# Second attention of a four-layer recurrent stack: queries projected once, two heads per matmul

## The chip, the cores and the metric

The kernel runs on one core of one Trainium2 chip. The metric is device microseconds of one execution, here the median of three runs. Engines are named as in the profile: PE is TensorE, DVE is VectorE, ACT is ScalarE, POOL is GpSimd, SP is SyncE, which issues the transfers.

## The reference, cut to what matters

The model has four layers. In each, an attention and a feed-forward part read the layer-normalised rows, and the product of the first and the gated second is added to the rows. There are 8192 rows of 128 numbers, worked on in 16 batches of 512. The change touches the attention of the second layer:

```
def _L1_attn_ref(x, Mq, Mk, Mv):
    HEADS = 8
    K_SIZE = 64
    B, C, _ = x.shape
    H, K = (HEADS, K_SIZE)
    V = Mv.shape[1] // H
    q = (x @ Mq).reshape(B, H, C, K)
    k = (x @ Mk).reshape(B, H, C, K)
    v = (x @ Mv).reshape(B, H, C, V)
    scores = jnp.einsum('bhqk,bhck->bhqc', q, k).reshape(B * H, C, C)
    att = jax.nn.softmax(scores / jnp.sqrt(jnp.float32(K)), axis=1)
    att4 = att.reshape(B, C, H, C)
    out = jnp.einsum('bqhc,bhcd->bqhd', att4, v)
    return out.reshape(B, C, H * V)
...
x = x + s * g
xn = _layernorm(x, axis=-1)
s = _L1_attn_ref(xn, L1_attn_Mq, L1_attn_Mk, L1_attn_Mv)
```

Here x is (16, 512, 128). The queries are reshaped without a transpose, so a head of the reference is a group of 64 consecutive rows with all 512 columns, and the softmax runs over the query axis. The kernel counts these groups as g and the eight blocks of 64 columns as s; in this document, as in the few words of the change, "head" means such a block of 64 columns.

## The kernel before, in words

`program` runs the phases of the four layers one after the other. The second attention is `paired_attention_phase`. Its loop goes over n = -1 to 16; the body of n computes the scores of batch n, prepares batch n + 1 and finishes batch n - 1. Each body has STEPS = 16 steps s = 8 rho + g. In a step TensorE issues two score matmuls that share one moment of the array (L582: key rows 0 to 63 on partitions 0 to 63, and 64 to 127 on the other half), each with 512 moving columns of queries, into one of two PSUM tiles of two banks, `scores_ps[s % 2]`. VectorE takes the maximum of both halves (`col_max`, L477), ACT the exponentials with their sums (`exps`, L437), VectorE the reciprocal (`invert`, L483), and GpSimd scales the probabilities in place (`scale_probs`, L404). The scores of step s wait for the exponentials of step s - 2, which free their PSUM tile.

Between the scores TensorE does the work of `misc_use` and `products`, in this order by step. Step 0 turns the normalised rows of the next batch (L111), which ACT copies to `rows.xT` and, twice side by side, to `xT_twice`. `project_k` (L613) makes keys in four parts, at the steps in K_AT; VectorE copies them (L488). `project_q` (L608) makes queries, one head of 64 columns at a time, at the steps in Q_AT; ACT scales and copies them into `q` (L427). The weights `wq` hold every head twice, so one matmul writes the same head into partitions 0 to 63 and 64 to 127, and both score matmuls find it on their half. Steps 9 and 10 turn the output of the batch before (L624), step 15 projects the values (L618). `products` (L601) adds up the weighted values of the first half of the keys in steps 10 to 13 and of the second half in steps 2 to 5 of the next body. All projections and turned outputs share two PSUM banks, `misc[s % 2]`; before a matmul overwrites one, TensorE waits for the copy that read its last content.

VectorE also forms the rows of batch n + 2 in steps 1 to 6: `sum_picks` (L500), `scale_s` (L505), `gate_s` (L509), which waits for a tanh on ACT (L447), `sum_x` (L514), then the moments (L92), and in step 11 `normalise` (L102). These stand in its queue between the maxima. The queue of SP holds, in each body: the four loads of batch n + 3, one weight load for the next phase, the store of the attention output of batch n - 1, a wait until it has landed, and the store of the rows of batch n + 2.

Of the kernel before, what the change touches and what calls it, by code (L numbers as in the profile page):

```python
# [163 lines left out]
def paired_attention_weights(nc, ctx, dram):  # L164
    S, W = 8, 64
    ahead = Ahead(nc, ctx, "a1", {"ident": [P, P], "wq": [D, S, 2, W], "wk": [D, 2, 2, 2, W], "wv": [D, D]})
    ident, wq, wk, wv = ahead.take("ident wq wk wv")
    ahead.loads = [(ident[:], dram["ident"]), (wv[:], dram["L1_Mv"])]
    ahead.loads += [(wq[:, :, twice, :], dram["L1_Mq"].rearrange("d (s w) -> d s w", s=S)) for twice in range(2)]
    k_columns = dram["L1_Mk"].rearrange("d (rho half a w) -> d rho half a w", rho=2, half=2, a=2)  # L170
    ahead.loads += [(wk[:, :, a, half, :], k_columns[:, :, half, a, :]) for a in range(2) for half in range(2)]
    return ahead
# [110 lines left out]
def paired_attention_phase(nc, tag, before_dram, x_dram, s_dram, routes, batches, ahead, following):  # L283
# [14 lines left out]
    Q_AT = {3: 0, 4: 1, 5: 2, 6: 3, 7: 4, 8: 5, 11: 6, 12: 7}  # L298
    K_AT = {1: 0, 2: 1, 13: 2, 14: 3}
    OUT_AT = {9: 0, 10: 1}  # L300

    with nc.cleanup_on_exit(), ExitStack() as ctx:
# [14 lines left out]
        q = sb("q", [P, 2, G, S, W])  # L317
# [14 lines left out]
        q_projected, q_ready = sem("q_projected"), sem("q_ready")  # L332
# [28 lines left out]
        def _(sp):  # L361
# [9 lines left out]

            load_parts(0)
# [3 lines left out]
            def body(j, n):  # L376
                if n <= LAST - 3:
                    load_parts(n + 3)
                following.load(sp, n - 1)
                if n >= 1:  # L380
                    b = j.plus(-1)
                    sp.wait_ge(s_ready, b.of(2, 2))
                    sp.dma_start(s_rows[b.number()], s_out[:]).then_inc(s_stored, 16)
                    sp.wait_ge(s_stored, b.of(16, 16))
                    sp.sem_inc(s_free, 1)
                if n <= LAST - 2:
                    store_x(n + 2)
# [29 lines left out]
        def _(act):  # L417
# [7 lines left out]
            def keep_q(b, buf, s, bank):  # L425
                act.wait_ge(q_projected, b.of(S, s + 1))
                act.activation(q[:, buf, :, s, :], grouped(bank), ACT.Copy,  # L427
                               scale=1.0 / math.sqrt(W)).then_inc(q_ready, 1)
# [22 lines left out]
            def body(j, n):  # L451
                for s in range(STEPS):
# [4 lines left out]
                    if n <= LAST - 1:  # L457
                        if s == 0:
                            keep_twice(j.plus(1))
                        if s in Q_AT:  # L460
                            keep_q(j.plus(1), (n + 1) % 2, Q_AT[s], misc[s % 2])
# [7 lines left out]
        def _(dve):  # L469
# [49 lines left out]
            def body(j, n):  # L519
                if n >= 0:  # L520
                    chain.restart()
                for s in range(STEPS):
# [19 lines left out]
                    if n <= LAST - 1 and s in K_AT:  # L542
                        keep_k(j.plus(1), (n + 1) % 2, K_AT[s], misc[s % 2])
# [3 lines left out]
                    if n >= 1 and s in OUT_AT:  # L547
                        at = OUT_AT[s]
                        dve.wait_ge(out_turned, j.of(2, at - 1))
                        if at == 0:  # L550
                            dve.wait_ge(s_free, j.of(1, 0))
                        dve.tensor_copy(s_out[:, :, at * 64:(at + 1) * 64].rearrange("p c (s d) -> p c s d", s=4),
                                        misc[s % 2][:].rearrange("p (c s d) -> p c s d", c=NC, s=4)[:, :, :, 0:DV]
# [15 lines left out]
        def _(pe):  # L569
            pe.sem_inc(products_done, 2)  # L570

            def scores(j, n, s):
                rho, g = divmod(s, G)
                if s == 0:
                    pe.wait_ge(q_ready, j.of(S, S))
# [51 lines left out]
            def misc_use(j, n, s):  # L627
# [7 lines left out]
                if s == 1 and nxt:  # L635
# [3 lines left out]
                    project_k(b, 0, misc[1])  # L639
                if s == 2 and nxt:  # L640
                    pe.wait_ge(twice_ready, b.of(1, 1))
                    project_k(b, 1, misc[0])
                if s == 3 and nxt:
                    pe.wait_ge(k_ready, b.of(4, 1))
                if s == 4 and nxt:
                    pe.wait_ge(k_ready, b.of(4, 2))
                if s in (5, 6, 7, 8) and nxt:
                    pe.wait_ge(q_ready, b.of(S, Q_AT[s - 2] + 1))
                if s in (11, 12) and nxt:
                    if n >= 1:  # L650
                        pe.wait_ge(s_ready, j.of(2, OUT_AT[s - 2] - 1))
                    else:
                        pe.wait_ge(q_ready, b.of(S, Q_AT[s - 4] + 1))
                if s in Q_AT and nxt:
                    project_q(b, Q_AT[s], misc[s % 2])
                if s in OUT_AT and n >= 1:
                    if nxt:
                        pe.wait_ge(q_ready, b.of(S, Q_AT[s - 2] + 1))
# [5 lines left out]
                    turn_out(n, OUT_AT[s], misc[s % 2])  # L664
                if s in (13, 14) and nxt:
                    pe.wait_ge(q_ready, b.of(S, Q_AT[s - 2] + 1))
                    project_k(b, K_AT[s], misc[s % 2])
                if s == 15 and nxt:
                    pe.wait_ge(k_ready, b.of(4, 4))
# [3418 lines left out]
```

## Time and profile before

| | |
|---|---|
| time, median of 3 runs | 6118.59 us (6117.81 to 6122.44) |
| span of the profiled execution | 6107.7 us |
| second attention, first scores to first scores of the last batch | 1260.03 to 1922.77 us |
| one batch of it | 44.06 us |
| PE busy over the span | 5688.7 us (93%) |
| DVE / ACT / POOL busy | 4318.9 (71%) / 3844.6 (63%) / 2914.7 us (48%) |
| DMA, mean over the span | 36 GB/s |

The page gives one profiled execution; a line such as L608 is a line of the kernel before. The second attention is about an eighth of the span, and its batches repeat, so it is read from one batch in order of time. In the rows below, a matmul in this number format is recorded as two matmuls, and a pair of score matmuls as four.

### The profile page before, as it was taken

What the parts mean: (1) busy time and instruction counts of PE and PEld (TensorE: products, weight loads), DVE (VectorE), ACT (ScalarE), POOL (GpSimd) and SP (SyncE); (2) the same over time, 40 slices, a digit from 0 to 9 for tenths busy, and PEclk for the clock granted to TensorE, in tenths of its full rate; (3) what the DMA queues carried; (4) which work ended last, traced back from release to release, by engine and by line L of the source; (5) the groups of instructions that cost most, each with busy time, mean ns of one, the idle gap of its engine ahead of it and who ended that gap; (6) DMA issues with size and microseconds to landing.
All of it is one profiled execution on the core that took longest, in us unless ns stands there. A gap on an engine that the chain in (4) does not pass through costs nothing. (4 is left out here: it accounts for less than half of the span.)

```text
span 6107.7 us, 102241 instructions
## 1 busy us (share of the span) xinstructions
PE 5688.7 (93%) x33833; PEld 3009.1 (49%) x33833; DVE 4318.9 (71%) x9755; ACT 3844.6 (63%) x8213; POOL 2914.7 (48%) x2774
## 2 busy tenths in 40 slices
PE   8999999779998999999999989999999999987868
PEld 3444444422222566666666634444444444445558
DVE  4555555177886777777788768888888888867655
ACT  2444444256665677777777757777777777756436
POOL 1224325457776766766666533323323323224458
PEclk9999999899999999999999989999999999999989
DMA  2001001211110111111111110000000000013123
GB/s 48 22 22 38 28 15 45 67 57 47 33 36 18 42 33 35 36 33 39 41 43 46 37 26 11 13 20 11 13 17 14 13 14 16 11 40 105 60 96 97
DMA packets 303981, 219.33 MB, mean 36 GB/s; under 512 B 27858, under 2 KB 279636, under 8 KB 302948
## 3 DMA queue, kind: packets, MB, share of 16 engines
q1 hardware_dynamic: 289332, 182.51, 11.2%
q0 software_dynamic: 12544, 29.71, 1.4%
q8 instruction: 275, 4.51, 0.3%
q14 instruction: 246, 2.02, 0.1%
q10 hardware_dynamic: 1584, 0.59, 0.0%
HBM read 97.11 MB, written 73.87 MB: 28 GB/s over the span
## 5 line engine op out<-in xcount | busy, mean ns | idle before, releaser
L3883 PE MATMUL a_scores_ps<-a_kT,a_q_mixed 128*128 128x512 f32 x2048 | 1046.4, 593 | 3.7 <-ACT a_probs L3695 3.1
L3893 PE MATMUL a_acc_ps<-a_probsT,a_v_post 128*128 128x512 f32 x2048 | 1042.8, 592 | 0.4 <-DVE a_probsT L3788 0.4
L3695 ACT ACTIVATE a_probs<-a_scores_ps,a_neg_max 128x512 f32<-128x512 f32 x1024 | 702.3, 686 | 429.5 <-DVE a_neg_max L3778 419.9
L3778 DVE TENSOR_REDUCE a_neg_max<-a_scores_ps 128x1 f32<-128x512 f32 x1024 | 692.9, 677 | 199.9 <-PE a_scores_ps L3883 194.2
L3788 DVE STREAM_TRANSPOSE a_probsT<-a_probs 128x512 f32<-128x512 f32 x1024 | 715.6, 699 | 136.6 <-PE a_acc_ps L3893 112.2
L3700 ACT ACTIVATE a_probs<-a_probs,a_inv_sum 128x512 f32<-128x512 f32 x1024 | 727.7, 711 | 0.8 <-DVE a_inv_sum L3783 0.8
L3096 DVE TENSOR_REDUCE a_neg_max<-a_pair_ps 128x2 f32<-128x1024 f32 (+3 forms) x512 | 417.5, 823 | 354.3 <-PE a_pair_ps L3192 347.8
L2901 ACT ACTIVATE a_probsT<-a_pair_ps 128x1024 f32<-128x1024 f32 (+3 forms) x512 | 359.0, 703 | 485.9 <-PE a_pair_ps L3205 469.0
L3893 PEld LDWEIGHTS a_acc_ps<-a_probsT,a_v_post 128*128 128x128 f32 x2048 | 389.0, 190 | 490.9 <-issue 488.8
L3883 PEld LDWEIGHTS a_scores_ps<-a_kT,a_q_mixed 128*128 128x128 f32 x2048 | 384.4, 190 | 476.6 <-issue 440.6
L3644 POOL TENSOR_TENSOR a_q_mixed<-a_qT,a_pre 128x512 f32<-128x512 f32 x248 | 250.0, 1040 | 759.7 <-PE a_scores_ps L3883 759.7
L404 POOL TENSOR_TENSOR a_probs<-a_probs,a_inv_sum 128x1024 f32<-128x1024 f32 x256 | 488.4, 1918 | 207.1 <-DVE a_inv_sum L483 206.9
L2862 POOL TENSOR_SCALAR_AFFINE_SELECT a_probsT<-a_probsT 128x256 f32<-128x256 f32 x512 | 209.6, 410 | 682.2 <-ACT a_probsT L2901 680.0
L437 ACT ACTIVATE a_probs<-a_scores_ps,a_neg_max 128x512 f32<-128x512 f32 x512 | 347.1, 684 | 241.9 <-DVE a_neg_max L477 240.7
L3652 POOL TENSOR_TENSOR a_v_post<-a_v,a_post 128x2048 f32<-128x2048 f32 x60 | 271.6, 4538 | 456.7 <-PE a_acc_ps L3893 332.6
L3192 PE MATMUL a_pair_ps<-a_k,a_q 32*128 32x512 f32 (+3 forms) x2048 | 436.5, 504 | 0.0
L3205 PE MATMUL a_pair_ps<-a_q_less,a_k 32*128 32x256 f32 (+3 forms) x2048 | 410.3, 487 | 27.9 <-DVE a_neg_max L3096 19.5
L978 ACT ACTIVATE f_probs<-f_s_ps,f_neg_max,f_q_norms 128x128 f32<-128x128 f32 x1024 | 386.2, 469 | 35.6 <-DVE f_neg_max L1126 35.1
L477 DVE TENSOR_REDUCE a_neg_max<-a_scores_ps 128x2 f32<-128x1024 f32 x256 | 312.7, 1222 | 126.0 <-PE a_scores_ps L582 120.9
L912 POOL TENSOR_TENSOR f_cos_part<-f_cos_part,f_sin_part 128x512 f32<-128x512 f32 x128 | 162.3, 1268 | 381.0 <-DVE f_sin_part L1111 381.0
L582 PE MATMUL a_scores_ps<-a_q,a_k 64*128 64x512 f32 x1024 | 293.2, 650 | 17.8 <-ACT a_probs L437 16.3
L1290 PE MATMUL f_k_ps<-f_w_qkv,f_hT 128*128 128x512 f32 x512 | 267.2, 604 | 6.7 <-DVE f_sin_part L1111 3.9
(420 smaller groups left out, 11852.0 us busy)
## 6 DMA issues: line engine op xcount, KB each, us to landing
f_v_even<-f_v_odd SPq DMA_DIRECT2D x224, 130.0 KB, 2.4
a_v<-a_v_rows SPq DMA_DIRECT2D x256, 64.0 KB
f_x_tiles<-routed_x SPq DMA_DIRECT2D x72, 193.0 KB
attention_out<-a_s_out SPq DMA_DIRECT2D x48, 256.0 KB, 2.3
routes_y_rows<-a_zeros SPq DMA_DIRECT2D x32, 256.0 KB
a_parts<-routes_y_rows SPq DMA_DIRECT2D x32, 256.0 KB, 3.5
f_x<-x_after SPq DMA_DIRECT2D x32, 256.0 KB, 2.8
f_gx<-x_after SPq DMA_DIRECT2D x32, 256.0 KB, 3.1
```

Of the source, the lines that this page charges most:

```text
L404: pool.tensor_tensor(units, units, inv_sum[:, s % 2].unsqueeze(2).to_broadcast([P, 2, S * W]), ALU.mult).then_inc(scaled, 1)
L978: last = act.activation(probs[:, hh, hp, :], score_ps[hh][:, hp * P:(hp + 1) * P], ACT.Exp, bias=neg_max[:, hh, hp:hp + 1], scale=q_norms[ ...
L2901: act.activation(probsT[:, g % NPT, 2 * rp:2 * rp + 2, 0:m], slot[:, :, 0:m], ACT.Exp).then_inc(probsT_ready, 1)
L3096: dve.tensor_reduce(neg_max[:, t, c, at:at + 33:32], ring[pair_of(n, 2 * s)][:, :, 0:m], AX.X, ALU.max, negate=True).then_inc(max_ready, 1)
L3192: last = pe.matmul(slot[:, a, 0:(c + 1) * P], q[r:r + 32, t, c * P:(c + 1) * P], k[r:r + 32, buf, t, p, 0:(c + 1) * P], start=False, stop= ...
L3205: last = pe.matmul(slot[:, a, 0:m], k[r:r + 32, n % 2, t, p, c * P:(c + 1) * P], q_less[r:r + 32, t, c * P:T], start=True, stop=True)
L3695: act.activation(probs[:, n % NPR, :], scores_ps[n % NS][:], ACT.Exp, bias=neg_max[:, n % NS:n % NS + 1], scale=1.0, accum_out=row_sum[:, ...
L3700: act.activation(probs[:, n % NPR, :], probs[:, n % NPR, :], ACT.Copy, scale=inv_sum[:, n:n + 1]).then_inc(probs_scaled, 1)
L3778: dve.tensor_reduce(neg_max[:, n % NS:n % NS + 1], scores_ps[n % NS][:], AX.X, ALU.max, negate=True).then_inc(max_ready, 1)
L3788: dve.transpose(probsT[:, g % NT, :, i * B32:(i + 1) * B32], probs[:, n % NPR, :].rearrange("p (i q) -> p i q", i=NI)).then_inc(probs_turn ...
L3883: pe.matmul(scores_ps[n % NS][:], q_mixed[:, g % 2, i].rearrange("f a q -> f (a q)"), kT[:, par, :], start=True, stop=True).then_inc(score ...
L3893: pe.matmul(acc_ps[par][:], v_post[:, g, i, :], probsT[:, g % NT, i, :], start=(p == 0), stop=(p == U - 1)).then_inc(products_done, 1)
```

## The change

Queries are projected once per pair of heads: `wq` holds eight heads side by side instead of each twice, and one matmul of 128 columns writes head 2m to partitions 0 to 63 and head 2m + 1 to the others. There are four projections per batch, not eight. ACT copies the result into slot 2m of `q`, whose axes change from (group, head, row) to (head, group, row). Then SP issues two transfers per pair: slot 2m of the first half of the partitions goes to slot 2m + 1 of the other half, and slot 2m of the other half to slot 2m + 1 of the first. So on the upper half each pair of heads stands in swapped order, and `products` reads `probs` at head `s ^ r`. TensorE waits for all eight transfers ahead of the first scores of a batch (`q_moved`). The steps of the projections and their banks are listed anew: queries at 3, 5, 6 and 7, keys at 1, 2, 8 and 12, and the waits that guard the two banks follow.

```diff
-    ahead = Ahead(nc, ctx, "a1", {"ident": [P, P], "wq": [D, S, 2, W], "wk": [D, 2, 2, 2, W], "wv": [D, D]})
+    ahead = Ahead(nc, ctx, "a1", {"ident": [P, P], "wq": [D, S // 2, 2 * W], "wk": [D, 2, 2, 2, W], "wv": [D, D]})
...
-    ahead.loads += [(wq[:, :, twice, :], dram["L1_Mq"].rearrange("d (s w) -> d s w", s=S)) for twice in range(2)]
+    ahead.loads += [(wq[:], dram["L1_Mq"].rearrange("d (m w) -> d m w", m=S // 2))]
...
-    Q_AT = {3: 0, 4: 1, 5: 2, 6: 3, 7: 4, 8: 5, 11: 6, 12: 7}
-    K_AT = {1: 0, 2: 1, 13: 2, 14: 3}
+    Q_AT = {3: 0, 5: 1, 6: 2, 7: 3}
+    K_AT = {1: 0, 2: 1, 8: 2, 12: 3}
     OUT_AT = {9: 0, 10: 1}
+    BANK = {0: 0, 1: 1, 2: 0, 3: 1, 5: 0, 6: 1, 7: 0, 8: 1, 9: 0, 10: 1, 12: 0}
...
-        q = sb("q", [P, 2, G, S, W])
+        q = sb("q", [P, 2, S, G, W])
...
+            def move_q(b, buf, m):
+
+                sp.wait_ge(q_ready, b.of(S // 2, m + 1))
+                first, other = q[0:W, buf], q[W:P, buf]
+                sp.dma_start(other[:, 2 * m + 1], first[:, 2 * m]).then_inc(q_moved, 16)
+                sp.dma_start(first[:, 2 * m + 1], other[:, 2 * m]).then_inc(q_moved, 16)
...
                 following.load(sp, n - 1)
+                if n <= LAST - 1:
+                    for m in range(S // 2):
+                        move_q(j.plus(1), (n + 1) % 2, m)
                 if n >= 1:
...
-            def keep_q(b, buf, s, bank):
-                act.wait_ge(q_projected, b.of(S, s + 1))
-                act.activation(q[:, buf, :, s, :], grouped(bank), ACT.Copy,
+            def keep_q(b, buf, m, bank):
+
+                act.wait_ge(q_projected, b.of(S // 2, m + 1))
+                act.activation(q[:, buf, 2 * m], grouped(bank), ACT.Copy,
...
-                    pe.wait_ge(q_ready, j.of(S, S))
+                    pe.wait_ge(q_ready, j.of(S // 2, S // 2))
+                    pe.wait_ge(q_moved, j.of(16 * S, 16 * S))
...
-                    last = pe.matmul(scores_ps[s % 2][:, half, :],
+                    last = pe.matmul(scores_ps[s % 2][:, half, :].rearrange("p (s t) -> p s t", s=S),
                                      k[rows_of, n % 2, rho, g].rearrange("p a t -> p (a t)"),
-                                     q[rows_of, n % 2, g].rearrange("p s t -> p (s t)"), start=True, stop=True)
+                                     q[rows_of, n % 2, :, g, :], start=True, stop=True)
...
-                                     probs[:, rho, r, :, s, :], start=(rho == 0 and r == 0),
+                                     probs[:, rho, r, :, s ^ r, :], start=(rho == 0 and r == 0),
...
-                pe.matmul(bank[:], wq[:, s].rearrange("d a w -> d (a w)"), rows.xT[:], start=True,
+                pe.matmul(bank[:], wq[:, s], rows.xT[:], start=True,
...
-                if s in (5, 6, 7, 8) and nxt:
-                    pe.wait_ge(q_ready, b.of(S, Q_AT[s - 2] + 1))
+                if s in (3, 5) and nxt:
+                    pe.wait_ge(k_ready, b.of(4, {3: 1, 5: 2}[s]))
+                if s in (6, 7, 8) and nxt:
+                    pe.wait_ge(q_ready, b.of(S // 2, s - 5))
...
-                    if nxt:
-                        pe.wait_ge(q_ready, b.of(S, Q_AT[s - 2] + 1))
+                    if nxt and s == 9:
+                        pe.wait_ge(q_ready, b.of(S // 2, 4))
+                    elif nxt and s == 10:
+                        pe.wait_ge(k_ready, b.of(4, 3))
...
+                if s == 12 and nxt:
+                    if n >= 1:
+                        pe.wait_ge(s_ready, j.of(2, -1))
...
                 if s == 15 and nxt:
+                    if n >= 1:
+                        pe.wait_ge(s_ready, j.of(2, 0))
                     pe.wait_ge(k_ready, b.of(4, 4))
```

## Rows read from the trace of the kernel before

**Rows 1.** Busy time by engine in one stretch: PE, PEld, DVE, ACT, POOL, granted clock, DMA.
```profile
1480.00:1524.00 44.00, 41.44 (x182) 12.76 (x180) 36.21 (x61) 29.15 (x77) 31.35 (x18) 1.00 0.14 39
```

**Rows 2.** Groups by line, 1240 to 1975 us: busy us, mean ns, idle before, releaser.
```profile
L477 DVE TENSOR_REDUCE a_neg_max<-a_scores_ps 128x2 f32<-128x1024 f32 x256 | 312.7, 1222 | 126.0 <-PE a_scores_ps L582 120.9
L608 PE MATMUL a_misc_ps<-a_xT,a_wq 128*128 128x512 f32 x256 | 142.6, 643 | 0.0
L601 PE MATMUL a_out_ps<-a_probs,a_v 128*32 128x512 f32 x1024 | 138.0, 614 | 5.7 <-POOL a_probs L404 5.7
...
L488 DVE COPY a_k<-a_misc_ps 128x512 f32<-128x512 f32 x64 | 43.1, 673 | 6.7 <-PE a_misc_ps L613 6.7
```

**Rows 3.** PE in order of time, one batch: start us, length us, instruction, idle before.
```profile
1479.61 1.13 PE L582 MATMUL a_scores_ps<-a_q,a_k 64*128 64x512 f32 x4
...
1484.12 1.10 PE L613 MATMUL a_misc_ps<-a_xT,a_wk 128*128 128x512 f32 x2 [1.74 <-ACT a_xT L116]
...
1497.59 1.13 PE L582 MATMUL a_scores_ps<-a_q,a_k 64*128 64x512 f32 x4
...
1515.40 1.13 PE L582 MATMUL a_scores_ps<-a_q,a_k 64*128 64x512 f32 x4
...
1518.52 1.13 PE L582 MATMUL a_scores_ps<-a_q,a_k 64*128 64x512 f32 x4
...
1520.63 1.13 PE L582 MATMUL a_scores_ps<-a_q,a_k 64*128 64x512 f32 x4
...
1523.67 1.13 PE L582 MATMUL a_scores_ps<-a_q,a_k 64*128 64x512 f32 x4
```

**Rows 4.** PE in order of time, last batch, steps 13 and 15.
```profile
1951.27 1.13 PE L582 MATMUL a_scores_ps<-a_q,a_k 64*128 64x512 f32 x4
...
1955.21 1.13 PE L582 MATMUL a_scores_ps<-a_q,a_k 64*128 64x512 f32 x4 [0.75 <-ACT a_probs L437]
```

**Rows 5.** ACT in order of time: the last sums of steps 4 and 12.
```profile
1496.68 0.20 ACT L437 ACTIVATION_READ_ACCUMULATOR a_probs<-a_scores_ps,a_neg_max 128x1 f32 x1
...
1516.90 0.20 ACT L437 ACTIVATION_READ_ACCUMULATOR a_probs<-a_scores_ps,a_neg_max 128x1 f32 x1
```

**Rows 6.** DVE in order of time: gate_s, normalise and the maximum of step 12.
```profile
1491.73 2.41 DVE L509 SCALAR_TENSOR_TENSOR a_parts<-a_gate,a_parts 128x512 f32<-128x512 f32 x1 [0.17 <-ACT a_gate L447]
...
1511.58 2.67 DVE L102 TENSOR_SCALAR a_xn<-a_x,a_moments,a_rstd 128x128 f32<-128x128 f32 x4
1514.39 1.23 DVE L477 TENSOR_REDUCE a_neg_max<-a_scores_ps 128x2 f32<-128x1024 f32 x1
```

**Rows 7.** POOL in order of time: two multiplies in a row.
```profile
1489.85 3.74 POOL L404 TENSOR_TENSOR a_probs<-a_probs,a_inv_sum 128x1024 f32<-128x1024 f32 x2 [1.96 <-DVE a_inv_sum L483]
```

**Rows 8.** Instructions of L509: ns shortest/median/longest, first and last start.
```profile
L509 DVE SCALAR_TENSOR_TENSOR a_parts<-a_gate,a_parts x16: 670/2408/2410, 1237.2 to 1845.9; 128x512 f32<-128x512 f32 x16
```

**Rows 9.** ACT and PE in order of time, ahead of the first batch.
```profile
1251.86 0.60 ACT L427 ACTIVATE a_q<-a_misc_ps 128x512 f32<-128x512 f32 x1 [0.36 <-PE a_misc_ps L608]
...
1255.49 0.60 ACT L427 ACTIVATE a_q<-a_misc_ps 128x512 f32<-128x512 f32 x1 [0.36 <-PE a_misc_ps L608]
...
1260.03 1.13 PE L582 MATMUL a_scores_ps<-a_q,a_k 64*128 64x512 f32 x4
```

**Rows 10.** Transfers between partition halves in the next phase: ns shortest/median/longest.
```profile
L836 SPq DMA_DIRECT2D f_v_even<-f_v_odd x96: 462/590/1820, 1990.3 to 3467.9; - x96
...
DMA to landing us min/median/max: 2.2/2.4/5.6
```

**Rows 11.** SP in order of time: the store of the attention output.
```profile
1509.36 0.37 SPq L383 DMA_DIRECT2D attention_out<-a_s_out  x1
```

**Rows 12.** PE busy time, granted clock, DMA in two stretches, and the scores that begin another batch.
```profile
1440.00:1444.00 4.00, 4.00 (x15) 0.72 0.00 0
...
1940.00:1944.00 4.00, 2.75 (x12) 1.00 0.00 0
...
1433.93 1.13 PE L582 MATMUL a_scores_ps<-a_q,a_k 64*128 64x512 f32 x4
```

More of the change, by code:

```diff
@@ L331, in paired_attention_phase @@
         pads = sem("pads")
-        q_projected, q_ready = sem("q_projected"), sem("q_ready")
+        q_projected, q_ready, q_moved = sem("q_projected"), sem("q_ready"), sem("q_moved")
         k_projected, k_ready = sem("k_projected"), sem("k_ready")
@@ L460, in body @@
                         if s in Q_AT:
-                            keep_q(j.plus(1), (n + 1) % 2, Q_AT[s], misc[s % 2])
+                            keep_q(j.plus(1), (n + 1) % 2, Q_AT[s], misc[BANK[s]])
                     if n >= 1 and s == PV_LAG + 3:
@@ L542, in body @@
                     if n <= LAST - 1 and s in K_AT:
-                        keep_k(j.plus(1), (n + 1) % 2, K_AT[s], misc[s % 2])
+                        keep_k(j.plus(1), (n + 1) % 2, K_AT[s], misc[BANK[s]])
                     if n >= 1 and s == PV_LAG + 3:
@@ L552, in body @@
                         dve.tensor_copy(s_out[:, :, at * 64:(at + 1) * 64].rearrange("p c (s d) -> p c s d", s=4),
-                                        misc[s % 2][:].rearrange("p (c s d) -> p c s d", c=NC, s=4)[:, :, :, 0:DV]
+                                        misc[BANK[s]][:].rearrange("p (c s d) -> p c s d", c=NC, s=4)[:, :, :, 0:DV]
                                         ).then_inc(s_ready, 1)
@@ L638, in misc_use @@
                     pe.wait_ge(rows.xT_ready, b.of(1, 1))
-                    project_k(b, 0, misc[1])
                 if s == 2 and nxt:
                     pe.wait_ge(twice_ready, b.of(1, 1))
[L642 to L646, printed above, removed]
-                if s in (5, 6, 7, 8) and nxt:
-                    pe.wait_ge(q_ready, b.of(S, Q_AT[s - 2] + 1))
[L649 to L655, printed above, removed]
+                if s in (3, 5) and nxt:
+                    pe.wait_ge(k_ready, b.of(4, {3: 1, 5: 2}[s]))
+                if s in (6, 7, 8) and nxt:
+                    pe.wait_ge(q_ready, b.of(S // 2, s - 5))
                 if s in OUT_AT and n >= 1:
-                    if nxt:
-                        pe.wait_ge(q_ready, b.of(S, Q_AT[s - 2] + 1))
+                    if nxt and s == 9:
+                        pe.wait_ge(q_ready, b.of(S // 2, 4))
+                    elif nxt and s == 10:
+                        pe.wait_ge(k_ready, b.of(4, 3))
                     elif n == LAST:
@@ L663, in misc_use @@
                     pe.wait_ge(outT_kept_act if OUT_AT[s] == 0 else outT_kept, j.of(1, 1))
[L664 to L667, printed above, removed]
+                    turn_out(n, OUT_AT[s], misc[BANK[s]])
+                if s == 12 and nxt:
+                    if n >= 1:
+                        pe.wait_ge(s_ready, j.of(2, -1))
+                    else:
+                        pe.wait_ge(q_ready, b.of(S // 2, 4))
+                if s in Q_AT and nxt:
+                    project_q(b, Q_AT[s], misc[BANK[s]])
+                if s in K_AT and nxt:
+                    project_k(b, K_AT[s], misc[BANK[s]])
                 if s == 15 and nxt:
+                    if n >= 1:
+                        pe.wait_ge(s_ready, j.of(2, 0))
                     pe.wait_ge(k_ready, b.of(4, 4))
```

## The prediction

> **What bounds the kernel now.** I read the groups by line first, for the stretch of the second attention, then one batch in order of time on each engine, then the few waits inside it. The table of that batch says that TensorE is busy 41.44 of 44 us at the full granted clock, with the others well under it [rows 1]. The groups say what fills it: score matmuls, the query projections of L608 and the weighted sums of L601 [rows 2]. In order of time one batch takes 1523.67 - 1479.61 = 44.06 us [rows 3], and TensorE idles for long in one place of it, 1.74 us in step 1, where the key projection waits for ACT's xT copy [rows 3]. So the list of matmuls sets the time of this stage, unless a second bound lies close behind it.
>
> It does. Scores go to two PSUM tiles in turn, so the scores of step s wait for the exponentials of step s-2. In the last batch, which projects nothing, that loop is bare: scores of step 13 at 1951.27, of step 15 at 1955.21, behind a wait for ACT [rows 4]: 3.94 us for two steps, 1.97 each. On TensorE a step with a projection costs 2.11 us (1518.52 to 1520.63), so scores and a projection take a slot of 1.06 each; with a weighted sum too it costs 3.11 (1515.40 to 1518.52) [rows 3]. A weighted sum alone leaves 2.06, just above the loop; nothing beside the scores leaves 1.06, and there the loop decides.
>
> **Part by part.**
> *Projections.* Eight matmul pairs of L608 become four. 142.6 us of L608 for 128 projections [rows 2] is 1.11 us each by busy time, 1.06 from start to start. In effect steps 4, 11, 13 and 14 lose theirs, since key parts 2 and 3 move from steps 13 and 14 to 8 and 12, where queries 5 and 7 stood. At most 4 x 1.055 = 4.22 us leave the 44.06. What is late next takes some of it back:
> Step 6. Its scores stood at 1497.59 [rows 3] and could stand at 1496.53. They need the exponentials of step 4, whose second sum ends at 1496.88 [rows 5]. Those wait for a maximum that is queued behind the gate product, begun at 1491.73 and 2.41 us long [rows 6]; the scores that this maximum reads come before the removed matmul, so none of it moves. So scores 6 come at about 1496.9: 0.69 gained, 0.36 lost.
> Step 14. Steps 11 and 13 are worth 1.06 each, so the scores at 1518.52 could stand at 1518.52 - 0.69 - 2.11 = 1515.72. They need the exponentials of step 12, done at 1517.10 [rows 5], whose maximum at 1514.39 waits for the normalisation at 1511.58, 2.67 us long [rows 6]. That chain hangs on the maximum of step 11 and so moves by 0.69 only: 1516.41. Gained 2.07, lost 0.73 more.
> Step 15. Its scores could come one slot behind those of step 14, at 1517.5. They need the exponentials of step 13. Maximum 12, at 1513.70, takes 1.22, the key copy that now stands behind it in VectorE's queue 0.67 [rows 2], so maximum 13 starts at 1515.6. From the start of a maximum to the end of its exponentials it is 2.71 us (1514.39 to 1517.10), so 1518.3 in place of 1520.63: gained **2.33 us per batch**, down to 41.73.
>
> Both long VectorE operations are long because GpSimd is running: the gate product takes 2.41 us while L404 holds 1489.85 to 1493.59 [rows 7], and its shortest run is 0.67 [rows 8]. The gate product starts hundredths after L404's first multiply has ended, and its median of 2408 ns over 16 says it loses nearly every time [rows 8]. The steps ahead of it don't change, so I let it lose again. The Trainium skill (SBUF — State Buffer, "SBUF: two separate sides") says that VectorE and GpSimd take a shared pair of ports as an exclusive lock for the whole instruction, whoever starts first; the trace agrees as far as 2.41 against 0.67 goes. By that rule the outcome hangs on a hundredth of a microsecond, and the sum would be that of the first rival if VectorE won both.
>
> *Batches at the ends.* 13 batches run the full set (1 to 13): 13 x 2.33 = 30.3. Batch 0 has no weighted sums in steps 2 to 5, so its step 4 falls on the loop and gives nothing: 2.33 - 0.69 = 1.6. Batch 14 has neither gate nor normalisation and pays the bare loop alone in steps 14 and 15 (3.94 - 3.11 = 0.83): 4.22 - 0.83 = 3.4. Batch 15 projects nothing and stays.
>
> *Start.* Ahead of batch 0 projections alternate with ACT's copies of the queries; the fourth starts at 1251.86, the eighth at 1255.49 [rows 9]. Everything behind comes 3.6 us sooner, the first scores at 1256.4 in place of 1260.03.
>
> *Transfers.* New: eight per batch, 128 KB each, from one half of the partitions to the other. The nearest row is the next phase's copy of the same kind and size (130 KB): 0.46 to 0.59 us of SP's queue each, 2.2 to 5.6 us to landing, median 2.4 [rows 10]. The last copy of queries follows the exponentials of step 7. From scores 6 at 1496.9, one slot pair and the loop's 3.94 on, these end at about 1503, the copy by 1504.5 (an estimate), the last transfer is issued by 1505.5, landed by 1508 to 1511; the next batch's scores come at 1521.3. So the transfer costs nothing, with 10 us to spare. At the start there are few microseconds: the fourth copy ends at 1252.5, two issues and what the pair before has left put the last one at about 1253.4, landing 1255.6 at 2.2 and 1259 at 5.6, against 1256.4. I take 3.6 us for the start; the other bound is 1.0. On SP the waits for q_ready stand ahead of the store of s, store_x and the next loads. SP spent that time waiting for s anyway, until 1509.36 [rows 11], so nothing behind is late. The loads of batch 3 move a few microseconds, with a batch to spare.
>
> *The rest.* TensorE's new wait for q_moved holds its whole list, but its condition is 10 us old. The wait for s_ready at step 15 is met at step 10. ACT loses four copies a batch; in steps 6 to 8 it follows TensorE closely, so these copies were cover for nothing else, and I count 0. The queries are read as eight runs of 64 at a stride of 512 elements. L601 reads probs in just that pattern, 614 ns against 643 for contiguous L608 [rows 2]; the bounds are 0 and, if each score pair took one slot more, 1.06 us a pair. I take 0, since L601 is the nearest row. One weight load in the phase before is saved; it was issued some 100 us ahead of this stage, and I count nothing.
>
> *Clock.* In 4 of the 15 projecting batches (0, 4, 9, 14) the granted clock falls after the gap of step 1: the rows show one, 0.72 in a window, so part of it at the lower of the two levels, and that batch, begun at 1433.93, takes 45.68 us up to 1479.61, 1.62 more than its neighbour [rows 3, 12]. I leave that count; its bounds are 0 and 15.
>
> **Sum.** 30.3 + 1.6 + 3.4 + 3.6 = 38.9 us. The profiled execution spans 6107.7; it would span 6068.8. The median of the runs, 6118.59, stands 10.9 above the span, and so the forecast is 6118.6 - 38.9 = **6080 us**.
>
> **Rivals.**
> 1. *VectorE gets ahead of GpSimd*: gate product and normalisation run short, step 6 and 14 lose nothing and only the loop's 0.83 stays. 13 x 3.4 + 2.6 + 3.4 + 3.6 = 54 us, 6065. For it: a shift of hundredths decides. Against: the steps ahead don't shift. If TensorE alone decided, 15 x 4.22 + 3.6 = 67, 6052; the loop's 3.94 us speaks against it. Together 0.17.
> 2. *The clock falls in every batch*. 11 more batches at 1.62 take back 18 us: 6098. For it: three new short idles. Against: the last batch idles as long in its bare steps (0.75 us [rows 4]) and has the clock in full there, 1.00 from 1940 to 1944 with TensorE busy 2.75 of 4 us [rows 12]. The Trainium skill (TensorE: Matmul & The Clock Gate, "A second HAM failure mode: psum-queue depth-cycling") has short idles between groups of matmuls, often repeated, make the clock swing; no run here shows it in these steps. 0.10.
> 3. *GpSimd catches VectorE worse*: L404's sixteen multiplies, 1.87 us each [rows 7], now lie within 41.7 us, and the normalisation may be caught for longer. For a quarter of a multiply, 0.47 us per batch (an estimate), 13 x 1.86 + 8.6 = 33: 6086. 0.14.
> 4. *Slower*: the score matmuls pay for the strided queries. There are 256 pairs; 38.9 / 256 = 0.15 us per pair is where the gain is gone, and one slot each (1.06) makes 6351. L601 speaks against it. 0.03.
> 5. *The transfers come late*: they, and not the matmuls, release the scores of step 0 in each batch. From 10 us of extra landing time on it eats the gain; at 12.3, every batch of it, the time is that of before. 0.03.
>
> **How the numbers follow.** Forecast, within 6 us: 0.53. The range must hold rivals 1 to 3 but not 4 and 5: 6060 (between rival 1 and the full gain) to 6100. 0.2% is 12 us, about what a measurement can tell from no change; faster takes the forecast and rivals 1 to 3, less 0.02 for 2 and 3 adding up: 0.92. Same: that and rival 5, 0.05. Slower: rival 4, 0.03.
>
> **What would show it.** Right: L608 at 64 projections; a batch of 41.7 us; steps 4, 11 and 13 at 2.06 us; waits for ACT ahead of scores 6, 14 and 15 of about 0.3, 0.7 and 0.7 us; L582 no longer than before; no wait of TensorE for a transfer but at the start. Wrong: gate products of 0.7 us (rival 1), more windows under 0.9 in the granted clock (rival 2), normalisations above 2.8 us (rival 3), L582 longer (rival 4), scores 0 waiting for DMA (rival 5).

## The result and the profile after

| | before | after |
|---|---|---|
| median of the executions, us | 6120.51 (6117.81 to 6122.64) | 6076.56 (6071.75 to 6077.52) |
| ratio, 95% interval | | 0.9933 (0.9919 to 0.9946) |
| profiled execution, span, us | 6107.7 | 6075.6 |
| scores of step 0, batch 0 | 1260.03 | 1257.14 |
| scores of step 0, batch 15 | 1922.77 | 1887.35 |
| one undisturbed batch, us | 44.06 to 44.07 | 41.86 to 41.87 |
| projecting batches in which the clock falls | 4 of 15 | 5 of 15 |

The change is faster by 44 us on these medians, and by 37 in a later comparison (below). The traces say what of it belongs to the changed stage: from its first turns of x to its first scores 17.35 us before and 14.55 after, from there to the scores of the last batch 662.74 and 630.21. That is 2.8 and 32.5, together **35.3 us**. The rest is not in this stage's rows: in one series executions of the unchanged kernel lie 9 us apart (6111.82 to 6120.58), in another 23.

The groups by line of the kernel after, 1240 to 1940 us (busy us, mean ns, idle before, releaser), stand against [rows 2] and the score matmuls of before, the first row here (1240 to 1975 us):

```profile
L582 PE MATMUL a_scores_ps<-a_q,a_k 64*128 64x512 f32 x1024 | 293.2, 650 | 17.8 <-ACT a_probs L437 16.3
```

```profile
L489 DVE TENSOR_REDUCE a_neg_max<-a_scores_ps 128x2 f32<-128x1024 f32 x256 | 312.7, 1222 | 93.7 <-PE a_scores_ps L595 88.3
L595 PE MATMUL a_scores_ps<-a_q,a_k 64*128 64x512 f32 x1024 | 293.3, 650 | 44.4 <-ACT a_probs L449 42.9
L614 PE MATMUL a_out_ps<-a_probs,a_v 128*32 128x512 f32 x1024 | 138.7, 617 | 5.4 <-POOL a_probs L415 5.4
...
L621 PE MATMUL a_misc_ps<-a_xT,a_wq 128*128 128x512 f32 x128 | 72.2, 649 | 0.0
```

The query projections are halved, 142.6 to 72.2 us. The score matmuls, which now read eight runs of 64, take 650 ns and 293.3 us in all, and the row of before has 650 and 293.2 too. What is new is their idle time: 44.4 us, nearly all behind ACT's exponentials, where it was 17.8. So 70 us of matmuls went and 27 us of waiting came. The difference of these sums, 43, is not the gain: a matmul pair recorded as 1.13 us long is followed by the next after 1.06, so recorded lengths are a little too long and recorded waits a little too short.

Where it came shows in one undisturbed batch of TensorE in order of time (start us, length us, instruction, idle before and its releaser), to be held against [rows 3]:

```profile
1465.79 1.13 PE L595 MATMUL a_scores_ps<-a_q,a_k 64*128 64x512 f32 x4
...
1470.31 1.10 PE L626 MATMUL a_misc_ps<-a_xT,a_wk 128*128 128x512 f32 x2 [1.74 <-ACT a_xT L116]
...
1483.12 1.13 PE L595 MATMUL a_scores_ps<-a_q,a_k 64*128 64x512 f32 x4 [0.33 <-ACT a_probs L449]
...
1490.39 1.13 PE L595 MATMUL a_scores_ps<-a_q,a_k 64*128 64x512 f32 x4 [0.85 <-ACT a_probs L449]
...
1502.83 1.13 PE L595 MATMUL a_scores_ps<-a_q,a_k 64*128 64x512 f32 x4 [0.68 <-ACT a_probs L449]
1504.62 1.13 PE L595 MATMUL a_scores_ps<-a_q,a_k 64*128 64x512 f32 x4 [0.66 <-ACT a_probs L449]
...
1507.66 1.13 PE L595 MATMUL a_scores_ps<-a_q,a_k 64*128 64x512 f32 x4
```

The gap of step 1 is the old one. Steps 6, 14 and 15 wait 0.33, 0.68 and 0.66 us, where there was no wait; step 9 waits 0.85. And nowhere in the stage does TensorE wait for a transfer.

VectorE in the same batch, around the four waits:

```profile
1477.92 2.41 DVE L521 SCALAR_TENSOR_TENSOR a_parts<-a_gate,a_parts 128x512 f32<-128x512 f32 x1 [0.17 <-ACT a_gate L459]
1480.36 1.22 DVE L489 TENSOR_REDUCE a_neg_max<-a_scores_ps 128x2 f32<-128x1024 f32 x1
...
1487.41 0.32 DVE L97 TENSOR_SCALAR a_var_eps<-a_moments 128x4 f32<-128x4 f32 x1
1487.64 1.21 DVE L489 TENSOR_REDUCE a_neg_max<-a_scores_ps 128x2 f32<-128x1024 f32 x1
...
1497.25 2.67 DVE L102 TENSOR_SCALAR a_xn<-a_x,a_moments,a_rstd 128x128 f32<-128x128 f32 x4
1500.07 1.23 DVE L489 TENSOR_REDUCE a_neg_max<-a_scores_ps 128x2 f32<-128x1024 f32 x1
...
1501.28 0.67 DVE L500 COPY a_k<-a_misc_ps 128x512 f32<-128x512 f32 x1
1501.87 1.22 DVE L489 TENSOR_REDUCE a_neg_max<-a_scores_ps 128x2 f32<-128x1024 f32 x1
```

Ahead of each late maximum stands another operation: the gate product (2.41 us as in [rows 6]), the moments, the normalisation (2.67, as in [rows 6]) and the key copy. That is the order that the prediction read. That these are the cause, and not merely neighbours, is for the experiments.

### The profile page after: what moved, and what is told of

Its sections match the earlier page's. It is cut to its first block and busy times, and to the rows that moved or that the text cites. A ratio compares the mean times of both kernels' runs of the same rounds, so it can differ in the third digit from the quotient of the medians.

```text
span 6075.6 us, 102077 instructions
## 1 busy us (share of the span) xinstructions
PE 5628.7 (93%) x33705; PEld 2997.3 (49%) x33705; DVE 4321.5 (71%) x9755; ACT 3817.6 (63%) x8149; POOL 2917.5 (48%) x2774
## 5 line engine op out<-in xcount | busy, mean ns | idle before, releaser
L595 PE MATMUL a_scores_ps<-a_q,a_k 64*128 64x512 f32 x1024 | 293.3, 650 | 44.4 <-ACT a_probs L449 42.9
```

## The experiments

**The unchanged kernel again, and the changed one again.** The same two programs, to see what another execution gives.

> The kernel before, unchanged, profiled once more. The prediction took 10.9 us, the difference of the median of the runs (6118.59) and the span of the profile (6107.7), for something that lies around the span. In the four runs of the changed kernel the time is 1.9 us above the span (6077.52 and 6075.6). Theory A: the same 1.9 us holds here, and the profile shown was simply a shorter execution; then this span is its time less 1.9 us, and the 10 us lie in other phases, with batches of the second attention again at 44.06 us. Theory B: before has 9 us more around its span than after; then the span stays near 6107.7 beside a time near 6118.

Measured: 6116.72 us with a span of 6114.6, so 2.1 us lie around the span; in the executions profiled later it is 1.8 to 2.3. The steady batch is 44.06 to 44.07, first scores to last batch 662.65 (662.74 before). The 10.9 us that the prediction put around the span are not there: with about 2 us around its span of 6107.7, the profile shown of before was one of an execution some 9 us shorter than the median (an estimate). Of the 6.9 us between the two spans, 6.4 lie ahead of this stage (first turns of x at 1242.68 and at 1249.05).

> The changed kernel against the kernel before, in five rounds, to tell the saving to a few microseconds. By the profiles the second attention is shorter by 35.4 us (first scores of the last batch at 1887.35 against 1922.77) and the whole span by 32.1; by the medians so far it is 44. If the stage alone saves, and the rest only scatters, the ratio is 0.9942 (35.4 us) with an interval that holds it; if something outside the stage gains too, 0.9930 or less.

Measured: 6078.58 (6073.59 to 6080.07) against 6115.93 (6111.82 to 6120.58), ratio 0.9935 (0.9921 to 0.9948). Steady batch 41.85 to 41.86; first scores to last batch 627.28, which is 35.4 less than the unchanged kernel beside it; the start takes 15.81 us and not 17.55, 1.7 less: a gain of 37.1 for the stage, where the first pair of profiles gave 35.3. The steady batch is the same in both. The difference of 1.8 us goes with the granted clock: in the full batches it fell twice in the first profile of the unchanged kernel and three times in the second (1.7 us more gained), in batch 0 (1.1 more) and in the start (1.1 less) it took another course (below). Whole times scatter by several microseconds more.

**The transfers.** First the changed kernel without its eight transfers and the wait for them. Each score matmul reads the even head of a pair twice, so the odd heads are left out:

```diff
-                if n <= LAST - 1:
-                    for m in range(S // 2):
-                        move_q(j.plus(1), (n + 1) % 2, m)
...
-                    pe.wait_ge(q_moved, j.of(16 * S, 16 * S))
```

> The changed kernel without its eight transfers per batch and without the wait for them: each score matmul reads every even slot of the queries twice, so the odd heads are left out and their scores are those of another head; all instructions of the engines stay. Theory Q (the gain that is missing, 4.22 - 2.19 = 2.03 us per batch, stands in VectorE's queue): a batch stays at 41.87 us within 0.05, and only the start gets shorter, by at most 0.7 us (first scores at 1257.1, of which 0.7 were lost against 1256.4). Theory T (transfers cost it, by a wait or by contention): a batch falls below 41.6.

Then the other way round: the old kernel with the new layout of q, the strided read, and eight transfers of the same size per batch into a spare tile, with TensorE's wait for them:

```diff
-        q = sb("q", [P, 2, G, S, W])
+        q = sb("q", [P, 2, S, G, W])
+        spare = sb("spare", [P, S, G, W])
...
+                sp.dma_start(spare[W:P, 2 * m + 1], first[:, m]).then_inc(q_moved, 16)
+                sp.dma_start(spare[0:W, 2 * m + 1], other[:, m]).then_inc(q_moved, 16)
```

> The kernel before with eight projections as it was, but with the new order of the queries (so that the score matmuls read eight runs of 64 at a stride of 512) and with eight transfers of 128 KB per batch into a spare tile, for which TensorE waits ahead of the first scores of the next batch. Theory Q: the layout and the transfers cost nothing, a batch stays at 44.06 us within 0.05, the score matmuls at 650 ns. Theory T: a batch is longer than 44.3; the strided read alone would cost 16 times what each score pair grows by.

Measured without them: 6072.21 us, steady batch 41.86 to 41.87, with the same waits of 0.33, 0.85, 0.68 and 0.66. The start takes 15.83 us and the way to the last batch 627.44, against 15.81 and 627.28 with them, so the start isn't shorter either. With them alone: 6118.52 against 6115.93 for the unchanged kernel, a difference within its range, and a steady batch of 44.06 to 44.07. Its start is 18.46 us long and not 17.55, at a mean granted clock of 0.79 and not 0.85; no wait for a transfer stands in it. The group of score matmuls in the latter:

```profile
L595 PE MATMUL a_scores_ps<-a_q,a_k 64*128 64x512 f32 x1024 | 292.6, 649 | 19.9 <-ACT a_probs L449 18.4
```

649 ns, as with the contiguous read. Both the transfers and the stride are worth nothing per batch, to 0.01 us; rivals 4 and 5 are out.

**The old places.** The changed kernel, but key parts 2 and 3 stay at steps 13 and 14, and the four queries take steps 3 to 6:

```diff
-    Q_AT = {3: 0, 5: 1, 6: 2, 7: 3}
-    K_AT = {1: 0, 2: 1, 8: 2, 12: 3}
+    Q_AT = {3: 0, 4: 1, 5: 2, 6: 3}
+    K_AT = {1: 0, 2: 1, 13: 2, 14: 3}
```

> The changed kernel with half the projections, but the later key parts left where they stood before: queries at steps 3, 4, 5, 6, keys at 1, 2, 13, 14. Theory Q: what a projection gives back depends on the step it leaves. Steps 7, 8, 11 and 12 lose theirs; 7 and 8 are then bare and run on the loop, and the moments in front of the maximum of step 7 wait no longer for TensorE but hold it: a batch of 42.8 us in place of 41.87 (estimate from the same walk through the steps), with the waits for ACT ahead of scores 8 and 9 at 0.8 and 2.3 us together. Theory L (only the count of matmuls and the loop of two score tiles matter): four projections less give the same time, 41.87 us.

Measured: 6118.06 us, against 6114.17 for the unchanged kernel beside it, one execution each: half of the projections gone, and no gain in the time. By the trace the stage is 4.2 us shorter than that of the unchanged kernel run again (15.13 + 660.83 against 17.55 + 662.65), 2.4 of it in the start. Full batches last 44.07 to 44.32, two of them 45.54. Both expectations missed the total. One batch of TensorE in order of time:

```profile
1369.60 1.13 PE L595 MATMUL a_scores_ps<-a_q,a_k 64*128 64x512 f32 x4 [0.79 <-ACT a_probs L449]
1372.70 1.44 PE L595 MATMUL a_scores_ps<-a_q,a_k 64*128 64x512 f32 x4 [1.98 <-ACT a_probs L449]
...
1375.12 1.95 PE L595 MATMUL a_scores_ps<-a_q,a_k 64*128 64x512 f32 x4
...
1378.58 1.13 PE L595 MATMUL a_scores_ps<-a_q,a_k 64*128 64x512 f32 x4
...
1386.55 1.13 PE L595 MATMUL a_scores_ps<-a_q,a_k 64*128 64x512 f32 x4 [0.68 <-ACT a_probs L449]
```

and the table by stretch (stretch, its length, busy PE, PEld, DVE, ACT, POOL, granted clock, DMA) around step 1, around step 9 and over the batch:

```profile
1351.59:1359.59 8.00, 7.49 (x32) 2.05 (x34) 7.89 (x10) 4.60 (x12) 4.09 (x3) 1.00 0.00 0
1371.59:1379.59 8.00, 6.88 (x28) 2.40 (x28) 4.17 (x8) 5.06 (x15) 7.40 (x5) 0.79 0.10 23
...
1347.59:1391.71 44.12, 38.94 (x174) 12.10 (x173) 36.27 (x60) 27.19 (x74) 31.46 (x18) 0.96 0.28 72
```

The waits came as expected: steps 7 and 8 are bare, the loop lags by 0.79 and then by 1.98 us. Behind the 1.98 us the granted clock falls, and the next score matmuls are 1.44 and 1.95 us long instead of 1.13. From scores 9 to scores 11 it takes 1378.58 - 1372.70 = 5.88 us; in the changed kernel the same steps take 1579.65 - 1575.18 = 4.47 in a batch at the full clock. So the fall costs 1.41 us here, and 44.12 - 1.41 = 42.71 is what the waits alone would give, 0.1 under the expectation that counted them. The clock falls in each of the batches 1 to 14, in some behind step 1, in others behind step 9, and in the two of 45.54 behind both. So rival 2 of the prediction is real: it didn't come in the changed kernel, but in this neighbour of it. Against the changed kernel's 41.87 the new places of queries and keys are worth 0.84 us in waits and 1.41 in clock.

**What the three long waits hang on.** The prediction has the maxima queued behind other work of VectorE; the rival is the bare loop of scores, maximum and exponentials, which wouldn't care. Three edits of the changed kernel, each taking one operation from in front of a maximum. First gate_s a step later, at 5, and sum_x at 6:

```diff
-                        if s == 4:
-                            gate_s(n + 2)
                         if s == 5:
+                            gate_s(n + 2)
+                        if s == 6:
                             sum_x(n + 2)
```

> The changed kernel with gate_s in step 5 and sum_x in step 6 of VectorE's list, in place of steps 4 and 5; nothing else moves. Theory Q: the maximum of step 4 no longer stands behind the gate product of 2.41 us, so the 0.33 us that TensorE waits ahead of scores 6 go, unless the gate product now holds the maximum of step 5 as long; a batch of 41.55 us. Theory L: the loop sets these steps, a batch stays at 41.87.

Measured: 6071.15 us, steady batch 41.32 to 41.33, 0.54 less. The gate product's durations (ns shortest, median, longest):

```profile
L521 DVE SCALAR_TENSOR_TENSOR a_parts<-a_gate,a_parts x16: 669/672/693, 1243.1 to 1817.0; 128x512 f32<-128x512 f32 x16
```

and TensorE from step 6 to step 9 in one batch:

```profile
1444.61 1.13 PE L595 MATMUL a_scores_ps<-a_q,a_k 64*128 64x512 f32 x4
...
1446.73 1.13 PE L595 MATMUL a_scores_ps<-a_q,a_k 64*128 64x512 f32 x4
...
1448.84 1.13 PE L595 MATMUL a_scores_ps<-a_q,a_k 64*128 64x512 f32 x4
...
1451.74 1.13 PE L595 MATMUL a_scores_ps<-a_q,a_k 64*128 64x512 f32 x4 [0.71 <-ACT a_probs L449]
```

The product now starts in an idle moment of GpSimd (at 1441.84, its next multiply at 1442.00) and runs 0.67 us in place of 2.41; the wait of step 6 is gone, and that of step 9 is 0.71 again. From start to start that is 0.40 and 0.14 us, the whole 0.54; the expectation had counted only the recorded 0.33 of step 6.

Second, key part 3 a step later, at 13, so that its copy no longer stands in front of maximum 13:

```diff
-    K_AT = {1: 0, 2: 1, 8: 2, 12: 3}
+    K_AT = {1: 0, 2: 1, 8: 2, 13: 3}
```

> The changed kernel with key part 3 in step 13 in place of step 12. TensorE's list is as long as before. Theory Q: its copy on VectorE no longer stands between the maxima of steps 12 and 13, which the normalisation has made late already; the wait ahead of scores 15 falls from 0.66 to about 0.2 us, a batch of 41.40 us. Theory L: scores, a projection and a weighted sum make step 13 longer and step 12 shorter by one slot each, no gain: 41.87.

Measured: 6066.36 us, steady batch 41.40 to 41.41, 0.46 less. Scores of steps 14 and 15:

```profile
1462.44 1.13 PE L595 MATMUL a_scores_ps<-a_q,a_k 64*128 64x512 f32 x4 [0.68 <-ACT a_probs L449]
1463.77 1.13 PE L595 MATMUL a_scores_ps<-a_q,a_k 64*128 64x512 f32 x4 [0.21 <-ACT a_probs L449]
```

0.68 stays, and 0.66 becomes 0.21. Third, the normalisation of batches 1 to 15 done by ACT at step 13 (scale rstd, bias from one more small multiply on GpSimd), away from VectorE:

```diff
+                    if s == 13 and n <= LAST - 2:
+                        normalise(n + 2)
...
-                        if s == 11:
-                            rows.normalise(dve, j.plus(2).number())
```

> The changed kernel with the normalisation of batches 1 to 15 done by ACT in step 13 (four activations with scale 1/sigma and bias -mean/sigma, the bias made by one small operation each on VectorE and GpSimd), in place of VectorE in step 11. Theory Q: the maximum of step 12 comes 2.7 us earlier, the wait ahead of scores 14 goes, that ahead of scores 15 stays at the bare loop's 0.8: a batch of 41.2 us. Theory L: the wait was the loop's and not the normalisation's: 41.87.

Measured: 6071.82 us, steady batch 41.52, 0.35 less where 0.67 was expected. Steps 6 to 15 of one batch:

```profile
1486.06 1.13 PE L611 MATMUL a_scores_ps<-a_q,a_k 64*128 64x512 f32 x4 [0.33 <-ACT a_probs L455]
...
1493.39 1.13 PE L611 MATMUL a_scores_ps<-a_q,a_k 64*128 64x512 f32 x4 [0.92 <-ACT a_probs L455]
...
1497.11 1.07 PE L630 MATMUL a_out_ps<-a_probs,a_v 128*32 128x512 f32 x8 [0.18 <-POOL a_probs L417]
...
1505.33 1.13 PE L611 MATMUL a_scores_ps<-a_q,a_k 64*128 64x512 f32 x4
1507.21 1.13 PE L611 MATMUL a_scores_ps<-a_q,a_k 64*128 64x512 f32 x4 [0.75 <-ACT a_probs L455]
```

The wait of step 14 is gone, so the normalisation was its cause. The edit's own small operations give half of it back: 0.07 more at step 9, 0.18 where a weighted sum waits for GpSimd, and 0.09 more at step 15.

**All three together**, with the moments moved from step 6 to step 10, behind the stretch that they delayed:

```diff
-    K_AT = {1: 0, 2: 1, 8: 2, 12: 3}
+    K_AT = {1: 0, 2: 1, 8: 2, 13: 3}
...
-                        if s == 6:
+                        if s == 10:
                             rows.moments_of(dve, chain, j.plus(2).number())
```

> The changed kernel with the three edits that e6, e7 and e8 tried alone (gate_s and sum_x a step later, key part 3 in step 13, normalisation on ACT in step 13) and the moments in step 10 in place of 6, where VectorE's maxima wait for TensorE. Theory Q: with nothing long ahead of a maximum, only the bare loop at steps 13 to 15 (0.3) and the gap of step 1 (1.74) are left of the waits; a batch of 39.4 us, 2.5 less than the changed kernel, so some 33 us less in all, near 6043. Theory C (the clock): shorter batches with the same gap of step 1 meet the lower clock more often, up to 1.6 us in each as in e5; then a batch is 40.5 to 41 and the time near 6060.

Measured: 6054.49 us (6051.76 to 6058.40) against 6118.92 (6106.14 to 6129.39), ratio 0.9899 (0.9879 to 0.9918), under the whole interval of the changed kernel. Its steady batch is 39.45 to 39.46 (expected 39.4), but 7 batches take 41.0 to 41.1. Two neighbouring batches, one of each kind, by stretch:

```profile
1381.14:1422.25 41.11, 38.80 (x172) 11.84 (x173) 32.55 (x58) 28.75 (x77) 32.05 (x19) 0.96 0.26 66
1422.25:1461.70 39.45, 37.15 (x172) 11.63 (x173) 32.44 (x58) 28.64 (x77) 32.00 (x19) 1.00 0.26 69
```

The same 172 matmuls take 1.65 us longer at a mean clock of 0.96. The expectation by the waits gave the batch, the one by the clock the rest of the total: seven falls of about 1.6 us are 11, and the time lies 11 above the 6043 of the waits alone, though whole times scatter by several microseconds.

**The moments one step later**, at 11, to take away the last wait, 0.41 us ahead of scores 13:

```diff
-                        if s == 10:
+                        if s == 11:
                             rows.moments_of(dve, chain, j.plus(2).number())
```

> As e9, with the moments in step 11. Theory Q: the bare loop of steps 13 to 15 is no longer met with a late maximum, a batch of 39.1 us, 6039; if GpSimd is behind with its multiplies, ACT waits for the small operations behind them in step 13, and the batch is longer than that of e9. Theory C as in e9.

Measured: 6053.77 (6048.28 to 6058.12), ratio 0.9896 (0.9876 to 0.9916), no other than the one before. The steady batch is longer, 39.96 to 39.97, as the expectation had it for a GpSimd that is behind: the normalisation now waits for GpSimd in ACT's queue,

```profile
1496.54 1.65 ACT L464 ACTIVATE a_xn<-a_x,a_shift_by,a_rstd 128x128 f32<-128x128 f32 x4 [0.63 <-POOL a_shift_by L429]
```

but only 3 batches lose the clock. Longer batches with fewer falls, and the same sum.

## Why the prediction was right, step by step

**Forecast.** 6080 us, measured 6076.56 and 6078.58. The 38.9 us of gain were worked out for the stage, and the stage's gain is 35.3 in one pair of profiles and 37.1 in the other. So the sum was 1.8 to 3.6 us too large, and that the total came within 4 us owes something to the scatter between executions. The term "10.9 us around the span" was wrong as a description (2.1, by the unchanged kernel run again); it did no harm, because it amounted to starting from the median.

**Projections and the three waits.** From one start of scores to the next, step 6 lost 0.40 us (1483.12 - 1479.61 = 3.51, where before it was 3.11; said 0.36), step 14 0.74 (0.73) and step 15 0.73 (0.80); the waits recorded, 0.33, 0.68 and 0.66, are each some 0.07 shorter. That they hang on VectorE's queue is shown by the edits that took away one of the three at a time; of the wait of step 15, 0.21 stays when the key copy goes. The gate product did lose to GpSimd in every undisturbed batch. The period is 41.87 instead of 41.73, and the 0.14 has one place, step 9, which was not on the list: 0.85 against 0.71 before. The nearest row is VectorE's small operation on the moments, here of before, behind the scores of step 9 of before:

```profile
1504.72 1.13 PE L582 MATMUL a_scores_ps<-a_q,a_k 64*128 64x512 f32 x4 [0.71 <-ACT a_probs L437]
```

```profile
1501.88 0.18 DVE L97 TENSOR_SCALAR a_var_eps<-a_moments 128x4 f32<-128x4 f32 x1
```

It takes 0.18 us there and 0.32 after, as the row of after shows, with a run of three GpSimd multiplies from 1481.74 to 1487.70 beside it: it ends at 1487.73. In every batch of the profiles of before and after it ends 0.02 to 0.04 us behind a multiply of GpSimd, and in the 26 full batches of the two profiles of the changed kernel it takes 0.31 to 0.32 us where step 9 waits 0.84 to 0.85, and 0.18 where it waits 0.71 to 0.72. The 0.14 us go straight into the next maximum. That they are the whole of it was not tried by itself; with the gate product moved, the wait is back at 0.71. The step of the prediction that didn't hold is that steps not named don't change: the later start of that operation relative to GpSimd's multiply is not in it, and it is worth 0.14 us per batch.

**Batches at the ends.** The full batches 1 to 13 gave 28.6 us (576.11 to 547.49) in the first pair and 30.4 (577.74 to 547.38) in the second, said 30.3. Thirteen undisturbed batches give 28.6 to 28.7; in the second pair three falls of the clock stand on each side and cost 1.6 us less in the changed kernel (below), so that 30.4 meets 30.3 is chance. Batch 14 gave 3.4 in both (44.93 to 41.54, and 43.28 to 39.88), as said. Batch 0 was to give 1.6 us. It gave that in the second pair, 41.63 to 40.02, where the clock fell behind step 1 in both kernels, but only 0.5 in the first, 41.70 to 41.18. It has no weighted sums in steps 2 to 5 to cover the loop, and the prediction followed one of these steps. The rows of the profile first shown of after, scores of steps 4 to 7:

```profile
1267.69 1.13 PE L595 MATMUL a_scores_ps<-a_q,a_k 64*128 64x512 f32 x4 [0.71 <-ACT a_probs L449]
1269.55 1.13 PE L595 MATMUL a_scores_ps<-a_q,a_k 64*128 64x512 f32 x4 [0.73 <-ACT a_probs L449]
...
1273.39 1.13 PE L595 MATMUL a_scores_ps<-a_q,a_k 64*128 64x512 f32 x4 [1.66 <-ACT a_probs L449]
...
1276.23 2.06 PE L595 MATMUL a_scores_ps<-a_q,a_k 64*128 64x512 f32 x4
```

Three waits, and the clock falls behind the third (the last row's matmul is 2.06 us long). In the second execution the clock fell earlier, behind step 1; the matmuls there were slower, and the waits of 0.73 and 1.66 didn't arise.

**Start.** Said 3.6, got 2.8 (and 1.7 in the second pair, where the stretch ran at a mean granted clock of 0.75 instead of 0.83). The bound of 1.0 for late transfers wasn't needed; what came late was a key copy. The rows of after, VectorE and then TensorE:

```profile
1253.16 1.11 DVE L102 TENSOR_SCALAR a_xn<-a_x,a_moments,a_rstd 128x128 f32<-128x128 f32 x4
1254.41 0.69 DVE L500 COPY a_k<-a_misc_ps 128x512 f32<-128x512 f32 x1
```

```profile
1255.16 2.05 PE L631 MATMUL a_misc_ps<-a_wv,a_xT_twice 128*128 128x128 f32 x16 [1.69 <-DVE a_k L500]
1257.14 1.13 PE L595 MATMUL a_scores_ps<-a_q,a_k 64*128 64x512 f32 x4
```

The normalisation of the next batch, which used to lie in idle time of VectorE, now stands ahead of the last key copy, and the value projection waits 1.69 us for it, 0.78 before. The difference, 0.91, covers the shortfall of 0.8 of the first pair. One of the experiments shows the cause: with the normalisation on ACT, the same projection waits as long as before,

```profile
1257.74 2.05 PE L647 MATMUL a_misc_ps<-a_wv,a_xT_twice 128*128 128x128 f32 x16 [0.79 <-DVE a_k L515]
```

and the start takes 13.70 us at the same mean clock of 0.83: 3.65 less than before, as forecast, and no transfer is waited for there either. "Everything behind comes sooner" forgot a second engine's queue.

**Transfers, stride, clock.** All counted at nothing, and nothing they are (without them 41.87, alone 44.06). For the clock the prediction kept four falls; there were five in one execution and four in the other, of 1.05 to 1.12 us in the full batches where 1.62 was the row. A disturbed batch shows why it is cheaper. VectorE's gate product there:

```profile
1520.29 0.67 DVE L521 SCALAR_TENSOR_TENSOR a_parts<-a_gate,a_parts 128x512 f32<-128x512 f32 x1
```

TensorE loses 1.59 us up to scores 3 (1517.90 - 1507.66 = 10.24, against 1559.23 - 1550.58 = 8.65 in an undisturbed batch). That delay lets the gate product start ahead of GpSimd's next multiply, so it runs short, step 6 has no wait and step 9 one of 0.72: rival 1's mechanism, in these batches alone and for the gate product alone (the normalisation keeps its 2.67). From start to start 0.40 and 0.14 us come back, which leaves the 1.05. In the kernel with the later gate product, which has no such wait to lose, a fall costs 42.91 - 41.33 = 1.58.

**Rivals.** 1 came by half, in the disturbed batches only; 2 not in the changed kernel, but in all batches from 1 to 14 of the kernel with the old places; 3 in the small form of step 9; 4 and 5 not at all.

## What to carry to other kernels

Before counting a removed matmul as time, follow the chain that feeds the slot it leaves, operation by operation in the queue of each engine: here 4.22 us of matmuls became 2.2 because VectorE served other work ahead of the maxima, and most of that could be bought back by moving one operation at a time, 0.54, 0.46 and 0.35 us of it. Where the work stands decides as much as how much there is: with the projections halved but two key parts left at their old steps, a full batch was no shorter. And when a stage is short of work on TensorE, look at the granted clock by batch, for the waits that replace the work can cost more than their own length.

## What the runs showed of the hardware

**The clock.** Waits of 1.66 to 1.98 us on TensorE, with the engine busy on both sides, stood directly ahead of the falls, in which the granted clock went from 1.00 to 0.79 in stretches of 8 us, so partly at the lower of its two levels (1.2 GHz). The same gap of 1.74 us in step 1 stands in every batch, and the clock fell behind it in some and not in the others. In the changed kernel, a batch with a fall and one without:

```profile
1511.00:1519.00 8.00, 6.83 (x21) 1.64 (x21) 7.35 (x8) 4.60 (x11) 4.09 (x3) 0.79 0.00 0
1469.00:1477.00 8.00, 6.69 (x26) 1.81 (x30) 7.90 (x10) 4.60 (x12) 4.09 (x3) 1.00 0.00 0
```

What decides between them stays open; TensorE's rows ahead of the gap are the same to some hundredths. The falls don't look strewn at random: in the unchanged kernel they lie, after that of batch 0, at batches 4, 9 and 14 in one profile and at 3, 8 and 13 in the other, five batches apart. The numbers differ by kernel, with one or two profiles each: of the 13 full batches 2 and 3 in the unchanged kernel, 3 and 3 in the changed one, 7 where the steady batch is 39.45, 3 where it is 39.97, all of them with the old places. The Trainium skill (TensorE: Matmul & The Clock Gate, "A second HAM failure mode: psum-queue depth-cycling") tells of a kernel in which short idles between groups of matmuls, as it cycled through PSUM, made the clock swing and cost throughput; the traces here agree in kind, at 1.4 to 1.65 us a fall.

**VectorE and GpSimd.** The gate product takes 0.67 us or 2.41, by which of the two engines starts first, and where it starts first, the multiply of GpSimd beside it takes 2.26 us in place of 1.89 (batch 6 of the changed kernel). An operation of only 128x4 elements is caught too: 0.17 us with GpSimd idle ahead of the first batch, 0.18 or 0.32 in the full batches and up to 1.06 in batch 0, each time ending just behind a multiply. The Trainium skill (SBUF — State Buffer, "SBUF: two separate sides") says that the pair of ports these two share is held by one of them for a whole instruction, and the rows agree for single instructions.
